# Attention row products on two halves of the matrix array, issued four at a time, with the side work moved to other tiles

## What is computed

```python
q, k, v = (proj(Wq), proj(Wk), proj(Wv))              # (B, H, S, D), H = 16, D = 16
scores = jnp.einsum('bhsd,bhtd->bhst', q, k) * scale
scores = jnp.where(mask[None, None, :, :], -jnp.inf, scores)
attn = jax.nn.softmax(scores, axis=-1)
out = jnp.einsum('bhst,bhtd->bhsd', attn, v)
out = out.transpose(0, 2, 1, 3).reshape(B, S, E)
out = out @ Wo.T                                      # then an RMS norm and a modulation
```

## Time and profile before

| | us |
|---|---|
| median of three runs | 1162.13 (1159.18 to 1162.16) |
| profiled execution, its time | 1156.71 |
| its span in the trace | 1154.8 |
| TensorE busy | 1115.1 (97%) |
| VectorE, ScalarE busy | 776.1, 790.7 |
| mean granted TensorE clock | 0.991 |

### The profile page before, as it was taken

The page is one execution under the profiler, slowest core; times in us unless marked ns, Lnnn a source line. Parts: engine busy times, 40 slices in busy tenths (PEclk is TensorE's granted clock), DMA queues, the critical chain, the costliest instruction groups (busy, mean ns, idle before and its releaser), DMA issues.

```text
span 1154.8 us, 23346 instructions
## 1 busy us (share of the span) xinstructions
PE 1115.1 (97%) x7466; PEld 779.2 (67%) x7520; DVE 776.1 (67%) x2265; ACT 790.7 (68%) x1752; POOL 511.7 (44%) x837
## 2 busy tenths in 40 slices
PE   8899999999999999998988999999999999999988
PEld 5333434435344353443438989999999999999968
DVE  5877778787887878877745435356555555668647
ACT  2478778787787877866794656656566656666645
POOL 7424135584755837557552465354222222222210
PEclk8999999999999999998999999999999999999999
DMA  8765738367383663844737588846566666723536
GB/s 209 211 191 189 223 101 254 121 224 232 117 276 123 221 209 120 269 139 127 262 106 271 136 291 304 262 122 144 161 188 201 202 193 193 215 49 69 165 91 219
DMA packets 101616, 213.64 MB, mean 185 GB/s; under 512 B 10917, under 2 KB 71341, under 8 KB 93046
## 3 DMA queue, kind: packets, MB, share of 16 engines
q1 hardware_dynamic: 86038, 192.42, 51.3%
q0 software_dynamic: 14304, 18.69, 9.0%
q10 hardware_dynamic: 1152, 1.05, 0.4%
HBM read 239.28 MB, written 74.29 MB: 272 GB/s over the span
## 4 chain that ended last, share of the span: by engine, by line
PE 45%; POOL 2%; DMA 2%; DVE 2%; issue 1%; ACT 1%; SPq 1%; POOLq 0%; ACTq 0%
PE bank L1101 38%; PE bank L1261 1%; PE bank L1116 1%; DMA x<-yout,rows 1%; PE bank L1130 1%; PE bank L1203 1%; PE bank L1221 1%; POOL routed L1980 1%; DMA routed<-xw,idx 0%; PE bank L1295 0%; PE bank L1184 0%; PE bank L1170 0%; PE bank L1241 0%; DMA w_parts<-in_W 0%; POOL run L862 0%
## 5 line engine op out<-in xcount | busy, mean ns | idle before, releaser
L1643 DVE CUSTOM_DVE_ANT_0 junk<-bank,mneg 128x512 bf16<-128x512 f32 x512 | 332.5, 683 | 105.4 <-PE bank L1170 104.9
L1369 ACT ACTIVATE pt<-bank 128x512 f32<-128x512 f32 x512 | 300.9, 595 | 65.5 <-PE bank L1184 31.9
L1990 POOL DMA_INDIRECT x<-yout,rows x78 | 122.5, 1570 | 291.2 <-ACT yout L1453 231.1
L1101 PE MATMUL bank<-hid,w 128*128 128x256 f32 x1872 | 244.7, 287 | 3.9 <-DVE hid L1791 3.9
L1101 PEld LDWEIGHTS bank<-hid,w 128*128 128x128 f32 x1872 | 231.4, 191 | 5.6 <-issue 4.3
L1791 DVE TENSOR_TENSOR hid<-full,hid 128x256 fp32r<-128x256 f32 x312 | 133.1, 430 | 139.1 <-ACT full L1448 137.9
L1443 ACT ACTIVATE hid<-bank,biases 128x256 fp32r<-128x256 f32 x312 | 149.9, 480 | 93.2 <-PE bank L1101 91.3
L1448 ACT ACTIVATE full<-bank,biases 128x256 f32<-128x256 f32 x312 | 149.2, 478 | 0.0
L1188 PE MATMUL bank<-mneg,identb 128*128 128x512 bf16 x332 | 126.4, 381 | 0.0
L1203 PE MATMUL bank<-pt,vaug 128*17 128x512 f32 x1024 | 124.0, 602 | 1.4 <-DVE turned L1670 0.5
L1101 PE MATMUL bank<-w,hid 128*128 128x256 f32 x936 | 121.9, 283 | 1.5 <-DVE hid L1791 1.5
(11 more groups left out here) (184 smaller groups left out, 1455.0 us busy)
## 6 DMA issues: line engine op xcount, KB each, us to landing
w<-split_weights SPq DMA_DIRECT2D x80, 1024.0 KB
w<-split_weights SPq DMA_DIRECT2D x40, 2048.0 KB
split_weights<-w_parts SPq DMA_DIRECT2D x64, 512.0 KB, 3.8
w_parts<-in_W SPq DMA_DIRECT2D x64, 256.0 KB, 4.6
split_parts<-parts SPq DMA_DIRECT2D x28, 384.0 KB, 2.6
rows<-routed SPq DMA_DIRECT2D x39, 258.0 KB, 3.7
stacks<-split_parts SPq DMA_DIRECT2D x36, 256.0 KB, 5.5
qst<-split_parts SPq DMA_DIRECT2D x24, 256.0 KB, 5.2
```

The costliest lines, as they stand in the source:

```text
L1101: product = T.matmul(ps, w[p], x[q], start=(k == 0 and n == 0), stop=(k == len(weights) - 1 and n == 2))
L1369: A.activation(pt[n % len(pt)][:, :], ps[:, :], ACT.Exp, scale=float(D) ** -0.5).then_inc(exped.sem, 1)
L1643: V.tensor_tensor_reduce(junk[n % 2][:, :], ring_bank(step)[0][:, :], mneg[:, 0, st, :], 1.0, FLOOR, ALU.add, ALU.max, rowmax[gi % 2][:, h ...
L1990: G.indirect_dma_start(x2_dram, bass.IndirectOffsetOnAxis(ap=rows[j % NS][:, tt, E + 1:E + 2].bitcast(U32), axis=0), yout[j % NY][:, tt], ...
```

## The change

1. A row product takes four of the six pairs only: 64 rows (`KR`), not 96. The maxima shift the exponent alone, and the column products keep all six pairs. Heads 0 and 1 of each group have these 64 rows on partitions 0 to 63 and heads 2 and 3 on 64 to 127 (`pair_rows`), so the column products of heads 2 and 3 run over 128 rows, 30 of them zeros. Heads are stored in another order (`slot_of`, `by_halves`).
2. The four row products of a tile follow one another (step `rows`), heads 0, 2, 1, 3, ahead of its four column products. Groups 0 and 1, which have no column products beside them, keep single row products in an order by halves.
3. The `project`, `project_v` and `project_o` steps stand in tiles with odd k alone (in the last tiles everywhere), and `rest` is the first step of the next tile, ahead of its row maxima on VectorE.
4. Transfers: a stack step has twice as many, of half the size; `mrow` goes in two. GpSimd's constants are eight memsets, not two.
5. The routing chain of a batch has other pauses, and starts sooner; seeds may be written three column products ahead, not two.

```diff
-FIRST_PROJECTS = range(3, 7)
+FIRST_PROJECTS = range(2, 6)
+ROW_PAIRS = 4
+KR = ROW_PAIRS * D
+ROW_HEADS = (0, 2, 1, 3)
-SEED_AHEAD = 2
+SEED_AHEAD = 3
...
+def pair_rows(half, r):
+    if r < ROW_PAIRS:
+        first, step = half * KR + r, ROW_PAIRS
+    else:
+        first, step = (KR, KR // 2)[half] + r - ROW_PAIRS, len(PAIRS) - ROW_PAIRS
+    return slice(first, first + (D - 1) * step + 1, step)
...
         out.append(("scale", b, st))
-        yield
+        for _ in range(2 if b < KNOWN - 1 else 1):
+            yield
...
-        if todo and todo[0][0] == "stack":
+        if todo and todo[0][0] in ("stack", "chain"):
...
+            if i >= 2 and rests:
+                step = rests.pop(0)
+                out.append(step)
+                parted.append(("part",) + step[1:])
+            if 2 <= i < GROUPS:
+                out.append(("rows", i, k))
...
+                if k % 2 and n == 1 and i >= 2 and todo and todo[0][0] != "project":
+                    work_off()
...
-            for _ in range(2 if len(todo) > 12 else 1):
-                if todo and i >= 2:
-                    work_off()
+            if todo and i >= 2 and (k % 2 or i >= GROUPS - 2):
+                work_off()
...
                     for r in range(n, len(PAIRS), STACK_STEPS):
-                        start((qst, kst)[qk][b % 2][r:KQ:len(PAIRS), :, :].rearrange("d (a h) s -> d a (h s)", a=2),
+                        for half in range(2):
+                            start((qst, kst)[qk][b % 2][pair_rows(half, r), half * (H // 2):(half + 1) * (H // 2), :],
...
+        def row_product(gi, hh, st):
+            b, half, at_slot = gi // NG, hh // 2, slot_of(gi % NG * GH + hh)
+            ps = take(ring_bank(("row", gi, hh, st)))
+            stacks_loaded(pe, b, half)
+            rows = slice(half * KR, (half + 1) * KR)
+            T.matmul(ps[:, :], qst[b % 2][rows, at_slot, st * P:(st + 1) * P],
+                     kst[b % 2][rows, at_slot, :], start=True, stop=True).then_inc(row_scored.sem, 1)
...
+            elif name == "rows":
+                gi, st = at
+                for hh in ROW_HEADS:
+                    row_product(gi, hh, st)
...
+                stack = slice(0, P) if hh // 2 else slice(0, KQ + SHIFTS)
...
+            for stacks in (kst, qst):
+                constant(G.memset, stacks[i][0:KR // 2, halves[1], :].bitcast(F32), 0.0)
+            for half in range(2):
+                constant(G.memset, kst[i][shift_rows_of(half), halves[half], :].bitcast(F32), TWO_MINUS_ONES)
```

More of the change, by code:

```diff
@@ L152, in chain @@
         out.append(("square_x1", b, st))
-        yield
+        for _ in range(2 if b < KNOWN - 1 else 1):
+            yield
     out.append(("root_x1", b))
-    for _ in range(4):
+    for _ in range(3 if b < KNOWN - 1 else 4):
         yield
@@ L288, in attention_order @@
     out.extend(value_steps(0))
+    first_rows = [(i, hh, st) for n in range(2) for i in range(2) for st in range(ST) for hh in (2 * n, 2 * n + 1)]
     for i in range(GROUPS + 3):
@@ L751, in _build @@
     ring_end = order.index(("layer1", 0, 0))
-    ring_users = [s for s in order[:ring_end] if s[0] in ("row", "col", *misc_stages)]
+    ring_users = []
+    for s in order[:ring_end]:
+        if s[0] == "rows":
+            gi, st = s[1:]
+            ring_users += [("row", gi, hh, st) for hh in ROW_HEADS]
+        elif s[0] == "one_row":
+            ring_users.append(("row", *s[1:]))
+        elif s[0] == "col" or s[0] in misc_stages:
+            ring_users.append(s)
     ring_place = {s: n for n, s in enumerate(ring_users)}
@@ L766, in _build @@
         for kt in range(ST):
[L767 to L772, removed]
+            choices = []
+            for hh in range(GH):
+                before_it = ring_before(("col", gi, kt, hh))
+                if before_it[0] == "col":
+                    choices.append((col_place[gi, kt, hh] - col_place[before_it[1:]], -hh))
+            if choices:
+                ahead, hh = max(choices)
+                place = col_place[gi, kt, -hh]
+                seed_after[cols_at[place - min(ahead, SEED_AHEAD)]] = gi, kt, -hh
     seeded = signal("seeded", [seed_after[at] for at in cols_at if at in seed_after])
@@ L983, in sync_program @@
                     sp.wait_ge(*last_col(b - 2))
-                start(qst[b % 2][KQ:KQ + SHIFTS, gi % NG * GH:(gi % NG + 1) * GH, :], mrow[gi % 2][:, :]).then_inc(dma_mrow[gi % 2], 16)
+                sp.wait_ge(constants_made, CONSTANTS)
+                for half in range(2):
+                    first, n = slot_of(gi % NG * GH + half * GH // 2), SHIFTS * GH // 2
+                    start(qst[b % 2][shift_rows_of(half), first:first + GH // 2, :],
+                          mrow[gi % 2][half * n:(half + 1) * n, :]).then_inc(dma_mrow[gi % 2], 16)
             elif name == "pads":
@@ L1642, in vector_program @@
                     dve.wait_ge(*max_split.at((gi - 2,)))
[L1643 removed]
+                V.tensor_tensor_reduce(junk[n % 2][:, :], ring_bank(("row", gi, hh, st))[0][:, :], mneg[:, 0, st, :], 1.0, FLOOR, ALU.add, ALU.max,
                                        rowmax[gi % 2][:, hh, st:st + 1]).then_inc(max_found.sem, 1)
@@ L1832, in constant, with shift_constants @@
             made[0] += 1
+        def shift_constants(i):
+            halves = [slice(half * (H // 2), (half + 1) * (H // 2)) for half in range(2)]
+            for stacks in (kst, qst):
+                constant(G.memset, stacks[i][0:KR // 2, halves[1], :].bitcast(F32), 0.0)
+            for half in range(2):
+                constant(G.memset, kst[i][shift_rows_of(half), halves[half], :].bitcast(F32), TWO_MINUS_ONES)
         G.memset(ident[:, :], 0.0).then_inc(ident_made, 1)
```

62 lines of the change are left out of this document (34 added, 28 removed).

## The result

The changed kernel took 1176.44 us (median of four runs, 1173.95 to 1179.44), the kernel before 1160.66 (four runs). The ratio is 1.0141, with a 95% interval of 1.0122 to 1.0160: slower by 1.4%, where I had forecast 1137 us and at most 1156.

What follows compares the result with a forecast made beforehand. TensorE, 97% busy, was taken as the bound: 1156.7 - 22.9 (pairs) - 1.8 (last groups) + 6 (waits) - 5.8 (handover) = 1132.2 for the profiled run, 1137.6 from the median of runs; 8-in-10 range 1116 to 1156 us.

Steps and rivals of the forecast that it cites:

- VectorE, ScalarE and the banks: Steady attention tiles: bursts on VectorE raise TensorE's idle time from 0.04 to 0.10 us a tile, 6 us lost.
- I count it nothing: VectorE's order in a tile: `rest` coming first shifts 0.6 us and costs nothing, inside the same waiting allowance.
- The pairs: Row products of each tile: two overlapping pairs cost 0.66 us for 0.88, 22.9 us gained in groups 2 to 27.
- The handover: From attention to the experts: the routing starts earlier, so the wait and slow clock there go, 5.8 us gained.
- The last row groups: Groups 28 to 31, 16 tiles: half of the pairs' 3.5 us is kept, 1.8 us gained.
- The covered edits: Constants, split transfers and 128-row column products: hidden behind other work, no time counted.
- Rival 2: Attention tiles: VectorE, ScalarE and banks take half back, 0.15 to 0.2 us a tile lost, 1153 us; chance 0.16.
- rivals for pairs that fail: Row bursts: halves take turns, 1182 us, chance 0.07; or pairs overlap only in part, 1149 to 1162, chance 0.10.

Runs made afterwards that it cites:

- e3: Kernel before plus only the side products in odd tiles and `rest` first on VectorE; row products single over 96 rows: ratio 0.9960.
- e6: e3 with the four row products of a tile in one unpaired burst ahead of the column products, with the changed kernel's seeding rule: ratio 1.0266.
- e9: Changed kernel with its seven banks handed out by a table instead of in turn; the choice of seeded column products changes too: ratio 1.0035.
- e13: Changed kernel with the burst behind the first column product of its tile, banks still in turn: ratio 0.9989.
- e8: Changed kernel with a projection behind the second column product of an odd tile, alone there, instead of at the tile's end: ratio 1.0051.
- e1: Changed kernel with `rest` behind the tile's first row maximum in VectorE's queue, not ahead of it: ratio 1.0197.
- e16: e11 without pairs: row products over 96 rows, one behind the other, with a bank table made for it: ratio 0.9995.
- e11: Changed kernel with the burst behind the first column product, `rest` behind the first row maximum, and banks by a table: ratio 0.9892.
- e17: Changed kernel with the burst behind the first column product and banks by a table, `rest` still first on VectorE: ratio 0.9927.
- e4: Changed kernel with a tile's four row products issued as two pairs, the second behind the second column product: ratio 1.0048.
- e7: e3 with the row products in two unpaired bursts of two, over 96 rows, with the changed kernel's seeding rule: ratio 1.0003.
- e12: Changed kernel with burst behind the first column product, banks by a table, and a projection behind an odd tile's second column product: ratio 1.0017.

## Why the prediction was wrong

**The step that failed** is "VectorE, ScalarE and the banks", where I allowed 0.06 us a tile, "6 us lost", with an upper bound of 0.2 a tile, 20 us. With the pairs' 0.24 off e3's tile of 4.49 a tile should take 4.25; it takes 4.63. So 0.38 a tile was lost, 40 us over 104 tiles, twice the bound. e6 shows 28 us lost over the same tiles without any pair (35 in the whole run), 6.8 of them to the clock; there TensorE idles for row maxima, and only 0.3 us for `rest`. With pairs the burst is over sooner, and 9.9 us of waits for `rest` come on top.

The working measured the wrong distance. It set the 3.2 to 3.4 us from one burst to the next against VectorE's 2.44 us of maxima. But banks are handed out in turn, and inside the same tile the fourth column product gets the bank of the burst's first row product, and behind a projection the third gets the projection's: 0.54 + two column products and masks, 1.4 us, for a copy and a subtraction on two engines. I had named the first of these ("the last column product of a tile waits for its first row maximum") and put no number to it. e9, which changes the banks alone (and the seeds with them), shows this path by itself: 14 us of the 40. e13 shows that another column product ahead of the burst is worth 19 us; that this is ScalarE kept in work, and one product more before the projection's bank is due, was only argued.

**"I count it nothing"** of `rest` first: in e3, with single row products, that holds. With the burst `rest` comes too late for the projection's bank: e8, which keeps `rest` first but gives that bank more time, gives back 12 us. VectorE's standing still (37.4 us) is not the price by itself: e3 has 39.9 us of it and loses nothing, and e1 takes it away and gains nothing.

**The pairs** (0.22 a tile): right, 0.23 by starts (e6) and 0.24 by busy time (e16 and e11, both near full clock). The Trainium skill, "TensorEngine Tiling (Array Packing)", Key Properties, warns of the drain at a change of tiling mode; the trace agrees, since two bursts with two changes each gain only 0.02 in busy time (4.45 to 4.43), 0.04 with seeds allowed for. That all of it would come off the time was wrong even in the best order, where 16 of 29 us return as waits.

**The handover** (5.8 us): near, 5.1. The wait ahead of `turn 1` is gone; `turn 0`, `turn 1` and `turn 2` start at

```profile
622.04 0.60 PE L1328 MATMUL bank<-ident,rows 128*128 128x128 f32 x4
...
632.67 0.60 PE L1328 MATMUL bank<-ident,rows 128*128 128x128 f32 x4
...
642.63 0.60 PE L1328 MATMUL bank<-ident,rows 128*128 128x128 f32 x4
```

20.6 us from first to last, before 25.7 (599.75, 614.74, 625.45), and e3 has 20.6 too. Only 2.5 us are left behind mark 31 because the way from that mark to `turn 0` is 0.7 us longer than before, and the way from `turn 2` to the end 1.9 (531.3 against 529.4; e3 529.2). What makes these longer I did not test.

**The last row groups**, where I had counted 1.8 us gained, lost 4.9. VectorE stands in front of a step of the routing table there while row products wait, then TensorE for row maxima, and the granted clock falls:

```profile
578.92 0.17 DVE L915 CAST tbi<-run 128x8 int32<-128x8 f32 x1 [3.24 <-POOL gt L915]
```

```profile
582.77 1.13 PE L1288 MATMUL bank<-wo,oT 128*128 128x256 f32 x4 [1.71 <-DVE rowmax L1710]
...
585.91 1.03 PE L1168 MATMUL bank<-kst,qst 64*128 64x512 bf16 x3 [1.16 <-DVE rowmax L1710]
```

```profile
560.00:600.00 40.00, 33.04 (x160) 10.71 (x156) 27.90 (x102) 22.12 (x49) 22.52 (x46) 0.83 0.52 192
...
586.00:590.00 4.00, 4.00 (x12) 1.21 (x13) 3.59 (x14) 1.94 (x4) 3.19 (x7) 0.50 0.28 99
```

No experiment took the table step out of that place, so its share is read from the trace and not shown. It isn't the step alone: e17 and e11 leave it where it is and take 68.2 and 67.1 us for these four groups, against 76.1.

**The covered edits** (constants, transfers, 128-row columns) cost little: e4, with all of them, differs from e7, with none, by 0.45%, and part of that is seeds (73 in 60 to 500 us against 84, each saving TensorE a mask). But they are not all covered: mark 1 stands at 52.7 us in e4 and 50.1 in e7, and at 52.0 in e11 and 48.5 in e16. Which edit of the first 50 us takes these 2.6 and 3.5 us was not tested.

**Rival 2** (half of the gain taken back, 1153) had the right mechanism and much too low a price. (Its sum takes 2 us for the handover where the forecast takes 5.8; with 5.8 it gives 1150.) I had given rivals for pairs that fail, and none for a burst that costs more than pairs give.

**Still open:** why e12 is slower than e17, how e13's 19 us divide between ScalarE's supply and the projection's bank, and what the burst of e6 costs TensorE apart from banks and clock.

## What to carry to other kernels

When products are gathered into a burst to save on an engine that is 97% busy, first list for every product behind the burst whose buffer it gets and when that one is read: a ring that fitted an alternating order here held a burst up on the oldest slot, though the readers were idle a quarter of the time. Try burst, saving and placement apart (a burst without the saving costs one run and here told most), and then the place of the burst and the order of the buffers before the saving is given up. Whether a consumer step may stand first in a queue depends on who asks for its buffer and how soon: the same order was harmless in e3, better than the other one with buffers in turn, and worse with a table.

## What the runs showed of the hardware

- Products of 64 rows on the two halves of the array overlap fully: two start together (258.67), the next two 0.22 us later. With coming and going four take 0.63 us, against 0.86 for four over 96 rows (e6, 252.20 to 253.06). The Trainium skill, "TensorE: Matmul & The Clock Gate", Measured speedup vs the span model, has 3.07 times for four row tiles, from which I had estimated 1.5 for a pair. The trace shows 2 for a pair by itself (0.22 us where two single products take 0.44), and 1.4 with coming and going inside (0.86 / 0.63).
- Coming and going cost about 0.2 us for both ways (0.63 - 0.44), close to what one pair saves: pairs in twos left TensorE's busy time nearly where it was.
- A wait of 1.7 us on TensorE (to 582.77) was followed by the clock's lower level, 1.2 GHz (0.54 from 584 to 585 us, 0.50 to 590), so that late banks cost more than they lasted. In e6 the two waits ahead of the fall near 202 us were 0.9 and 0.75 us long (to 200.02 and 201.17). In e6 the clock was 0.98 over all of 60 to 500 us, where every kernel with single products had 1.00.
